# The first half of a mixture-of-experts feed-forward made sparse: tokens sorted into 15 slot tiles, ahead of a dense second half

## The chip, the cores and the metric

The kernel runs on one core of one Trainium2 chip, as one program. The metric is the device time of one execution in microseconds (us), taken as the median over several executions. The engines are named as in the profile: PE is TensorE's matmul, PEld its weight load, DVE is VectorE, ACT is ScalarE, POOL is GpSimd, SP issues the DMAs. A q behind a name (PEldq) means the sequencer of that engine, which executes register instructions and sends the others on.

## The reference, cut to what matters

Three blocks follow each other on 1024 tokens of width 128: a bidirectional Mamba2 block, a cross attention of the 1024 tokens (8 heads) to 6404 context rows and themselves, and a feed-forward with 8 experts of hidden width 512, of which each token uses two. Only the last one changes:

```python
logits = xn @ router_w                       # 1024 x 8
topv, topi = jax.lax.top_k(softmax(logits), 2)
topv = topv / topv.sum(-1, keepdims=True)
comb = sum(one_hot(topi, 8) * topv[..., None], axis=1)
out = 0
for e in range(8):                           # every expert for every token, most with weight 0
    out = out + comb[:, e:e + 1] * swiglu(xn, gate_up_w[e], down_w[e])   # 128 -> 2 x 512 -> 128
out = out + swiglu(xn, shared_gate_up_w, shared_down_w)                  # 128 -> 2 x 128 -> 128
# swiglu: gate, up = split(x @ gu); silu(clip(gate, -10, 10)) * up @ dn
x = layernorm(x + out)
```

## The kernel before, in words

Each engine has an instruction list written out by hand, and semaphores order them. Every product of the feed-forward is made of three float16 matmuls (high x high, high x low, low x high).

**The attention** works through 16 blocks (head x half of the tokens, NBLK = 16), each of 30 steps (NS = 30). A step is six matmuls of 512 columns for the scores, two exponentials on ACT (`weights`), the low part on DVE (`low`), and, two steps later, six matmuls of 512 columns for the values. In a block, steps 0 to 6 and 25 to 29 (TAIL = 25) are written out, and steps 7 to 24 are a hardware loop of three turns (`Fori`). The addresses in these loops depend on registers, which FUSED_REGOPS and ALU_OP instructions of the PE sequencer work out between the matmuls. The last block (`end=True`) has no work for a following one, and carries the layer norm, the transposed copy and the routing of the first 512 tokens (`half_norm`, `turned`, `route`, in `half_in_block`).

**The feed-forward** runs over two halves of 512 tokens. A half is a shared unit, then 8 experts of 4 units each (hidden width 4 x 128), so 66 units in all. A unit u goes through a fixed chain:

- PE `gate_up`: three matmuls of 512 columns for the gate (bank u % 2), three for the up part (bank 2 + u % UPS, with UPS = 3). The gate waits until `clip` of unit u - 2 has read its bank, the up part until `hidden` of unit u - 3 has.
- DVE `clip` (L1447), ACT `silu` (L900), DVE `hidden` (L1455), ACT `high` (L906), POOL `hidden_low` (L617).
- An expert's down products are 4 tiles of 12 matmuls with 128 columns (`down`), two steps or more behind, into a ring of three banks (DOWNS = 3). DVE's `down_acc` (L1464) weighs each and adds it to `acc`, and frees its bank.

DVE's own order is: `clip(u)`, the tiles of the step before, `hidden(u - 1)`, then a piece of side work: the norm and routing of the second 512 tokens during the first half, the final norm of the first 512 during the second. PE places tiles behind the gate or the up part of given units (`tiles_at`): unit 0 of an expert has two, unit 1 none, units 2 and 3 one each. All PE matmuls are recorded under L1569.

Of the kernel before, what the change touches and what calls it, by code (L numbers as in the profile page):

```python
# [23 lines left out]
P = 128  # L24
# [32 lines left out]
UPS = DOWNS = 3  # L57
# [7 lines left out]
UNITS = 1 + 4 * E  # L65


def unit_of(half, e, i):

    return UNITS * half + 1 + 4 * e + i  # L70


def tile_of(half, e, t):

    if half:
        return 42 + 4 * e + t
    return 4 + 4 * e + t if isinstance(e, int) and e == 0 else 9 + t if isinstance(e, int) and e == 1 else 6 + 4 * e + t


def shared_tile(half, t):  # L80

    return 38 * half + t


TURNED, ROUTED = 8, 13
NTILES = tile_of(1, E - 1, HT - 1) + 1
ALL_TILES = range(HT)


def tiles_at(half, e, i):  # L90

    plain = {0: ([("own", -2, 2)], [("own", -2, 3)]), 1: ([], []), 2: ([], [("own", -1, 0)]), 3: ([], [("own", -1, 1)])}
    first = {(0, 0): {0: ([], []), 2: ([("shared", 0, 0)], [("shared", 0, 1)]), 3: ([("shared", 0, 2)], [("shared", 0, 3)])},
             (0, 1): {0: ([], [])},
             (0, 2): {1: ([], [("turned", 0, 0)])},
             (0, 3): {1: ([], [("routed", 0, 0)])},
             (1, 0): {0: ([], []), 1: ([], [("other", E - 1, 0)]), 2: ([], [("other", E - 1, 1)]),
                      3: ([("other", E - 1, 2)], [("other", E - 1, 3)])},
             (1, 1): {0: ([("shared", 0, 0)], [("shared", 0, 1)]), 1: ([("shared", 0, 2)], [("shared", 0, 3)])}}
    return first.get((half, e) if isinstance(e, int) else None, {}).get(i, plain[i])  # L100


BEFORE_SHARED = ([("other", E - 2, 2)], [("other", E - 2, 3)])
# [34 lines left out]
def layer(nc, a, out):  # L138
    ctx = ExitStack()
    with ctx:  # L140
# [47 lines left out]
        xf_1 = take([HT, D])  # L188

# [6 lines left out]
        U_sb = take([2, QB])  # L196

# [5 lines left out]
        A = take([4, 4, QB], F16)  # L203

# [118 lines left out]
        dn_ps, dn_acc, last_lo = sem("dn_ps"), sem("dn_acc"), sem("last_lo")  # L323
# [108 lines left out]

        def stage_parts(par, dst):
# [13 lines left out]
        def _(sp):  # L447
# [11 lines left out]
            loads(sp, ld_fv, fv)  # L459

# [5 lines left out]
            for e in range(E + 1):  # L466
# [17 lines left out]
        def _(pool):  # L484
# [130 lines left out]
            def hidden_low(u, k, lo, hi):  # L615
                pool.wait_ge(f_hi, u + 1)
                g.tensor_tensor(lo, hid[:, k % RING], hi, ALU.subtract).then_inc(f_lo, 1)  # L617

            def expert_low(half, e, par, blocks=4):
                for i in range(blocks):  # L620
                    hidden_low(unit_of(half, e, i), half + 1 + i, hlo[:, par, i], hhi[:, par, i])

            for half in range(2):
                hidden_low(UNITS * half, half, slo, shi)
                with pool.Fori(0, E // 2 - half) as pair:
                    for par in range(2):
                        expert_low(half, 2 * pair + par, par)
            for e in (E - 2, E - 1):
                expert_low(1, e, e % 2, 4 if e < E - 1 else 3)
# [3 lines left out]
        def _(act):  # L633
# [128 lines left out]
            def joint_act(h):  # L762
# [4 lines left out]
                if h:  # L767
                    act.wait_ge(ah_lo, h)
                s.activation(AH32[:], b[:, 0], ACT.Copy, scale=scale).then_inc(ah_f32, 1)
# [84 lines left out]
            def block_act(j, first=False, nxt=True, end=False):  # L854
# [6 lines left out]
                with act.Fori(0, LOOPN) as i:  # L861
                    for k in range(6):
                        weights(j, Turn(i, k))
# [1350 lines left out]
```

## Time and profile before

| | |
|---|---|
| median of 3 runs | 1809.35 us (1807.37 to 1809.6) |
| profiled execution | 1806.91 us, span of its instructions 1805.2 us |
| busy share of the span | PE 96%, DVE 83%, ACT 62%, PEld 48%, POOL 15% |
| last attention block | 1557 to 1660.6 us of the span |
| feed-forward, first half on PE | 1660.68 to 1726.1 us |
| feed-forward, second half on PE | 1726.1 to 1796.7 us |
| granted TensorE clock, mean | 0.991 |

Rows of the timeline give the start, the length, and how many like instructions were merged. A merged row's length ends with the modelled end of its last matmul, which lies behind the start of the next row: the distance of starts is the rate. A row of one source gives, per instruction and tile, the count, the shortest, median and longest duration in ns, and the first and last start.

### The profile page before, as it was taken

The page shows a single profiled execution, that of the slowest core. Times are in us where ns is not written, and L with a number is a line of the kernel's source. Part 1 is how long each engine was busy: PE and PEld are TensorE (multiplying, and loading weights), DVE is VectorE, ACT ScalarE, POOL GpSimd, SP SyncE. Part 2 cuts the span into 40 slices and gives each one's busy share as a digit, 9 for nine tenths or more (in the row PEclk, how much of TensorE's full clock was granted, in tenths as well). Part 3 has the DMA queues.
Part 4 walks back from the last instruction along what each step waited for, and adds up shares of the span by engine and source line. Part 5 has one row for each costly group of instructions (what it writes and reads, how often), then busy time and mean ns, then how long its engine had stood idle before and what let it go on. Part 6 is the DMA issues. An engine that isn't in the chain of part 4 may idle for free. (4 is left out here: it accounts for less than half of the span.)

```text
span 1805.2 us, 31230 instructions
## 1 busy us (share of the span) xinstructions
PE 1739.7 (96%) x9153; PEld 862.3 (48%) x9153; DVE 1492.3 (83%) x2398; ACT 1122.2 (62%) x1374; POOL 274.8 (15%) x340
## 2 busy tenths in 40 slices
PE   6977999999999999999999999999999999999998
PEld 4854444444444444444444444444444444444665
DVE  7968988888888888888878797979787888756987
ACT  4555566666666666666666666666666666676665
POOL 4846991000000000000000000000000000000554
PEclk9989999999999999999999999999999999999999
DMA  4001110000000000000000000000000000000000
GB/s 144 2 1 46 60 40 1 0 0 0 0 0 0 0 0 0 0 0 0 0 0 0 0 0 0 0 0 0 0 0 0 0 0 1 0 1 1 1 8 7
DMA packets 15381, 14.08 MB, mean 8 GB/s; under 512 B 5855, under 2 KB 13795, under 8 KB 14950
## 3 DMA queue, kind: packets, MB, share of 16 engines
q1 hardware_dynamic: 15334, 13.49, 2.5%
q8 instruction: 26, 0.43, 0.1%
q14 instruction: 21, 0.17, 0.0%
HBM read 12.96 MB, written 0.52 MB: 7 GB/s over the span
## 5 line engine op out<-in xcount | busy, mean ns | idle before, releaser
L833 ACT ACTIVATE p_arena<-PS 128x1024 f16<-128x1024 f32 (+1 forms) x480 | 484.4, 1009 | 529.5 <-PE PS L1569 529.3
L1569 PE MATMUL PS<-a_arena,z_arena 128*128 (+1 forms) x2832 | 746.4, 380 | 4.3 <-DVE a_arena L1253 4.1
L1569 PE MATMUL PS<-p_arena,z_arena 128*128 128x512 f16 x2800 | 740.4, 379 | 1.4 <-ACT p_arena L843 0.3
L1266 DVE TENSOR_TENSOR p_arena<-p_arena 128x1024 f16<-128x1024 f32 (+1 forms) x480 | 574.2, 1196 | 110.1 <-ACT p_arena L836 99.5
L1234 DVE TENSOR_REDUCE mxs<-PS 128x512 f32 (+1 forms) x900 | 581.8, 667 | 86.6 <-PE PS L1569 83.2
L836 ACT ACTIVATE p_arena<-PS 128x1024 f32<-128x1024 f32 (+1 forms) x480 | 481.9, 1004 | 0.0
L1569 PEld LDWEIGHTS PS<-a_arena,z_arena 128*128 (+1 forms) x2832 | 275.0, 98 | 332.4 <-DVE a_arena L1253 4.4
L1569 PEld LDWEIGHTS PS<-p_arena,z_arena 128*128 (+1 forms) x2800 | 269.2, 98 | 312.1 <-ACT p_arena L843 8.8
L1569 PE MATMUL PS<-z_arena,a_arena 128*128 (+3 forms) x1024 | 353.9, 361 | 10.5 <-DVE mxs L1234 8.2
L617 POOL TENSOR_TENSOR z_arena<-z_arena 128x512 f16<-128x512 f32 x65 | 75.3, 1160 | 1438.8 <-ACT z_arena L906 1438.5
L1569 PEld LDWEIGHTS PS<-z_arena,a_arena 128*128 (+1 forms) x1024 | 97.9, 98 | 143.7 <-DVE mxs L1234 26.4
L1569 PE MATMUL PS<-w_arena,z_arena 128*128 128x128 f16 (+1 forms) x856 | 67.4, 225 | 6.8 <-DVE w_arena L1110 2.7
L1569 PEld LDWEIGHTS PS<-w_arena,z_arena 128*128 128x128 f16 (+1 forms) x856 | 58.9, 105 | 25.0 <-POOL z_arena L617 5.5
L900 ACT ACTIVATE z_arena<-z_arena 128x512 f32<-128x512 f32 x66 | 41.6, 630 | 33.7 <-DVE z_arena L1447 33.4
L1447 DVE TENSOR_SCALAR z_arena<-PS 128x512 f32<-128x512 f32 x66 | 45.4, 688 | 16.1 <-PE PS L1569 14.6
L906 ACT CAST z_arena<-z_arena 128x512 f16<-128x512 f32 x66 | 40.7, 618 | 15.1 <-DVE z_arena L1455 15.1
L1569 PE MATMUL PS<-z_arena,w_arena 128*128 128x512 f16 x198 | 48.6, 379 | 0.0
L1569 PE MATMUL PS<-wt_arena,w_arena 128*128 128x512 f16 x198 | 48.0, 379 | 0.0
L1455 DVE SCALAR_TENSOR_TENSOR z_arena<-PS,z_arena 128x512 f32<-128x512 f32 x66 | 44.8, 679 | 1.5 <-ACT z_arena L900 1.3
L1569 PE MATMUL PS<-w_arena 128*128 128x64 f32 (+5 forms) x268 | 37.5, 281 | 7.3 <-DVE w_arena L1016 4.5
L1424 DVE TENSOR_REDUCE mxs<-PS 128x2 f32<-128x1024 f32 (+1 forms) x30 | 34.3, 1185 | 10.4 <-PE PS L1569 10.2
L546 POOL TENSOR_SCALAR p_arena<-p_arena,mv,rs 128x127 f32<-128x127 f32 x50 | 41.9, 850 | 0.0
(272 smaller groups left out, 924.0 us busy)
## 6 DMA issues: line engine op xcount, KB each, us to landing
w_arena<-in_L_ffn_gate_up_w SPq DMA_DIRECT2D x8, 512.0 KB, 3.7
p_arena<-in_ctx SPq DMA_DIRECT2D x2, 1600.0 KB, 9.1
w_arena<-in_L_ffn_down_w SPq DMA_DIRECT2D x8, 256.0 KB, 4.0
a_arena<-in_L_xattn_Wkv SPq DMA_DIRECT2D x1, 1024.0 KB, 5.8
w_arena<-in_x SPq DMA_DIRECT2D x1, 512.0 KB, 4.1
a_arena<-in_L_xattn_Wo SPq DMA_DIRECT2D x1, 512.0 KB, 6.8
w_arena<-in_L_xattn_Wq SPq DMA_DIRECT2D x1, 512.0 KB
out<-m_arena SPq DMA_DIRECT2D x4, 64.0 KB, 1.6
```

What stands on the lines that cost most here:

```text
L546: g.tensor_scalar(ctx_sb[:, c, 1:P], ctx_sb[:, c, 1:P], mv[:, c, 0:1], rs[:, 3, c:c + 1], ALU.subtract, ALU.mult).then_inc(z_scaled, 1)
L617: g.tensor_tensor(lo, hid[:, k % RING], hi, ALU.subtract).then_inc(f_lo, 1)
L833: s.activation(Phi[:, r % 3, 0:w], ps, ACT.Exp, scale=1 / SSC).then_inc(hi_ready, 1)
L836: s.activation(P32[:, r % 2, 0:w], ps, ACT.Exp, scale=1 / SSC).then_inc(p32_ready, 1)
L900: s.activation(sil[:, k % RING], gcl[:, k % RING], ACT.Silu, scale=1 / (XS * WS)).then_inc(f_silu, 1)
L906: s.copy(dst, hid[:, k % RING]).then_inc(f_hi, 1)
L1234: v.tensor_reduce(mxs[:, i, bass.ds(kb, 1)], PS[:, 6 + par, 0:w], AX.X, ALU.max).then_inc(mx_read, 1)
L1266: v.tensor_tensor(Plo[:, r % 3, at:w], P32[:, r % 2, at:w], Phi[:, r % 3, at:w], ALU.subtract).then_inc(lo_ready, 1)
L1424: v.tensor_reduce(mxs[:, i:i + 2, kb:kb + 1], PS[:, pair % 2 * 2:pair % 2 * 2 + 2, 0:w], AX.X, ALU.max).then_inc(mx_read, 2)
L1447: v.tensor_scalar(gcl[:, k % RING], PS[:, u % 2], lim, -lim, ALU.min, ALU.max).then_inc(f_clip, 1)
L1455: v.scalar_tensor_tensor(out=hid[:, k % RING], in0=PS[:, 2 + u % UPS], scalar=HS / (XS * WS), in1=sil[:, k % RING], op0=ALU.mult, op1=ALU. ...
L1569: return t.matmul(o, l, r, start=start, stop=stop)
```

## The change

**Sorting.** In the last attention block, the routing of the first half moves from steps 25 to 29 up to steps 7 to 17. New DVE work (`hot`, seven pieces) counts with two small matmuls how many of the 512 tokens, each taken twice, go to each expert, and gives each of the 1024 token copies a row in a list sorted by expert, where each expert's part begins at a multiple of 128. At most 15 tiles of 128 rows come out; all 15 are always worked on. A row holds the token's input (high and low part), its number and its weight (516 bytes). POOL sends the rows to DRAM in 8 indirect DMAs, SP reads them back in 3 DMAs, PE turns them tile by tile. The expert numbers of the 15 tiles are packed into two words that PE loads into registers. Steps 7 to 24 of this block are written out instead of looped. An internal DRAM tensor is set to zero early in the kernel (`xg_zero`).

**The first half.** It is now one shared unit and 15 slot units in a row. A slot unit is all of one expert's hidden width (4 blocks of 128) for 128 rows: 12 matmuls of 128 columns for the gate, 12 for the up part, with the weights at an address made of the expert's register; 12 more for the down product y, also by register; and 8 that scatter y back to the four token tiles through a 0/1 matrix that DVE makes (`choice`), all 15 summed in PSUM bank 7 (COMB). Per two slots, four matmuls turn the rows.

**Around it.** Bank 7 is needed for that sum, so UPS goes from 3 to 2. The second half keeps its matmuls (1 shared and 32 dense units), with tiles at the same places. Before unit 0, DVE does six pieces of the second half's norm. The first half's sum and final norm (`half_done`) follow in five double pieces during units 21 to 25.

```diff
-UPS = DOWNS = 3
+UPS, DOWNS = 2, 3
+COMB = 7
...
+SLOTS = 15
+WEAVE = False
+AHEAD = SLOTS
+def unit_order():
+    order, k = [("shared", 0, 0)], AHEAD
+    order += [("slots", i, 0) for i in range(AHEAD)] + [("shared", 1, 0)]
+    for e in range(E):
+        for i in range(4):
+            order.append(("dense", e, i))
...
+def small_work():
+    for half in range(2):
+        p = at_unit("shared", half)
+        for t in ALL_TILES:
+            put(p + 3 + t // 2, t % 2, "shared", half, t)
+    put(2, 1, "turned", 1, 0)
+    put(5, 1, "routed", 1, 0)
+    for f in range(2, (SLOTS + 1) // 2):
+        put(at_unit("slots", 2 * f) - 4, 1, "rows", f, 0)
+    for k in range(SLOTS):
+        p = at_unit("slots", k)
+        put(p + 3, 0, "y", k, 0)
+        put(p + 5, 1, "comb", k, 0)
+    for e in range(E - 1):
+        p = at_unit("dense", e, 3)
+        for t, (step, part) in enumerate(((3, 1), (4, 1), (5, 0), (5, 1))):
+            put(p + step, part, "own", e, t)
...
@@ gpsimd
+            for k in range(2):
+                for t in ALL_TILES:
+                    g.indirect_dma_start(xg_dram, bass.IndirectOffsetOnAxis(ap=posu[:, k, t:t + 1], axis=0),
+                                         xrow_f[:, k, t, :], None).then_inc(sent, 16)
@@ sync
+            sp.wait_ge(sent, 16 * 2 * HT)
+            for k, r in enumerate(SLOT_PARTS):
+                sp.dma_start(xg_f[:, r.start:r.stop, :],
+                             xg_dram.rearrange("(i p) n -> p i n", p=P)[:, r.start:r.stop, :]).then_inc(xg_ld[k], 16)
@@ vector
+                elif kind == "y":
+                    choice(a)
+                    dve.wait_ge(y_hi, a + 1)
+                    v.scalar_tensor_tensor(out=yw[:, a % 3, 1], in0=PS[:, bank, 0:P], scalar=xg_f[:, a, D + 1:D + 2],
+                                           in1=yw[:, a % 3, 0], op0=ALU.mult, op1=ALU.subtract).then_inc(dn_acc, 1)
...
+            for piece in range(6):
+                half_norm(1, piece)
+            for u in range(NUNITS):
+                clip(u)
+                if u:
+                    for kind, a, t in work_at(u - 1, 0) + work_at(u - 1, 1):
+                        small_dve(kind, a, t)
+                    hidden(u - 1)
+                side_work(u)
@@ tensor, last block
+                        if st == 10:
+                            pe.wait_ge(cnt_ready, 1)
+                            mm(PS[:, 6, 0:HT * E], J32[:], of_all)
+                            mm(PS[:, 6, HT * E:2 * HT * E], ones[:], of_all).then_inc(hot_ps, 1)
+                        elif st == 12:
+                            half_rows(xfhi[0], 7).then_inc(hot_ps, 1)
+                        elif st == 13:
+                            half_rows(xflo[0], 6).then_inc(hot_ps, 1)
...
+                    if st == TAIL and end:
+                        pe.wait_ge(hot_read, 3)
+                        for f in range(2):
+                            slots_turned(f, 6 + f).then_inc(xt_ps, 1)
+                    if st == TAIL + 3 and end:
+                        pe.wait_ge(et_ready, 1)
+                        packs.extend(t.value_load(packu[0:1, i:i + 1], min_val=0, max_val=E ** E - 1) for i in range(2))
@@ tensor, feed-forward
+            expert = [(packs[k // E] >> (3 * (k % E))) & (E - 1) for k in range(SLOTS)]
+            def free_bank(u, o):
+                if o == 0 and u >= 2:
+                    pe.wait_ge(f_clip, u - 1)
+                if o == 1 and u >= UPS:
+                    pe.wait_ge(f_hid, u + 1 - UPS)
+            def slots_products(u, o, blk, bank):
+                k = ORDER[u][1]
+                hi, lo = (w[:, bass.ds(expert[k] * (2 * F) + (F * o + blk * P), P)] for w in GU_flat)
+                c = bank[:, blk * P:(blk + 1) * P]
+                mm(c, hi, xt[:, k, 0], stop=False)
+                mm(c, hi, xt[:, k, 1], start=False, stop=False)
+                last = mm(c, lo, xt[:, k, 0], start=False)
```

## Rows read from the trace of the kernel before

**Rows 1.** The page's busy line, and one stretch of the chain (start, length)

```profile
PE 1739.7 (96%) x9153; PEld 862.3 (48%) x9153; DVE 1492.3 (83%) x2398; ACT 1122.2 (62%) x1374; POOL 274.8 (15%) x340
...
1740.58 46.92 PE PS L1569 x432
```

**Rows 2.** Busy time by stretch: the last attention block, the first half; PE, PEld, DVE, ACT, POOL, PEclk

```profile
1557.00:1660.60 103.60, 99.98 (x493) 48.61 (x492) 60.08 (x113) 71.51 (x77) 0.00 (x0) 1.00 0.00 1
1660.60:1726.00 65.40, 62.74 (x536) 38.49 (x535) 58.20 (x156) 42.16 (x69) 35.33 (x31) 1.00 0.00 1
```

**Rows 3.** What PE waited for, 1660 to 1700 us, then 1700 to 1790

```profile
PE PS L1569 <- POOL z_arena L617: 1.2, 2, 0.7
PE PS L1569 <- DVE acc L1464: 0.9, 1, 0.9
...
PE PS L1569 <- POOL z_arena L617: 0.6, 1, 0.6
```

**Rows 4.** Timeline of PE in the feed-forward: tiles of 12 narrow matmuls between wide ones

```profile
1701.10 0.83 PE L1569 MATMUL PS<-w_arena,z_arena 128*128 128x128 f16 x12
...
1701.77 0.81 PE L1569 MATMUL PS<-wt_arena,w_arena 128*128 128x512 f16 x3
...
1702.41 0.83 PE L1569 MATMUL PS<-w_arena,z_arena 128*128 128x128 f16 x12
```

**Rows 5.** Two sources by operation, 595.9 to 596.8 us: PE's sequencer in an attention loop

```profile
L1569 PEldq FUSED_REGOPS  x6: 46/46/60, 596.0 to 596.6; - x6
...
L1879 PEldq ALU_OP  x1: 32/32/32, 596.7 to 596.7; - x1
```

**Rows 6.** Timeline of an expert's units 1 and 2 in the second half

```profile
1747.30 2.75 PE L1569 MATMUL PS<-z_arena,w_arena 128*128 128x512 f16 x12
...
1748.22 0.69 DVE L1447 TENSOR_SCALAR z_arena<-PS 128x512 f32<-128x512 f32 x1
1748.83 0.60 DVE L1464 SCALAR_TENSOR_TENSOR acc<-PS,wt_arena,acc 128x128 f32<-128x128 f32 x2
1749.34 0.68 DVE L1455 SCALAR_TENSOR_TENSOR z_arena<-PS,z_arena 128x512 f32<-128x512 f32 x1
```

**Rows 7.** Timeline of the start of the feed-forward

```profile
1660.68 4.70 PE L1569 MATMUL PS<-wt_arena,w_arena 128*128 128x512 f16 x21
...
1661.61 0.68 DVE L1447 TENSOR_SCALAR z_arena<-PS 128x512 f32<-128x512 f32 x1
...
1664.03 0.86 DVE L1290 BATCH_NORM_STATS2 st<-acc 128x6 f32<-128x128 f32 x4
...
1666.13 0.37 DVE L1294 BATCH_NORM_AGGREGATE mv<-st 128x2 f32<-128x6 f32 x4
```

**Rows 8.** Small DVE operations of the norm, in order (1749.94 us and on)

```profile
1749.94 0.15 DVE L1305 TENSOR_TENSOR rs<-wt_arena 128x4 f32<-128x4 f32 x1
1750.13 0.16 DVE L1306 TENSOR_TENSOR rs<-rs,wt_arena 128x4 f32<-128x4 f32 x1
```

**Rows 9.** Timeline of steady steps in the last attention block

```profile
1601.26 1.46 PE L1569 MATMUL PS<-a_arena,z_arena 128*128 128x512 f16 x6
...
1603.68 1.02 ACT L836 ACTIVATE p_arena<-PS 128x1024 f32<-128x1024 f32 x1
1603.85 1.46 PE L1569 MATMUL PS<-a_arena,z_arena 128*128 128x512 f16 x6
1604.73 1.23 DVE L1266 TENSOR_TENSOR p_arena<-p_arena 128x1024 f16<-128x1024 f32 x1 [1.36 <-ACT p_arena L836]
```

**Rows 10.** DMA issues: KB each, median us to landing

```profile
w_arena<-in_x SPq DMA_DIRECT2D x1, 512.0 KB, 4.1
...
out<-z_arena SPq DMA_DIRECT2D x4, 64.0 KB, 1.6
```

**Rows 11.** Groups by operation, 1660 to 1806 us (busy, mean ns, idle before)

```profile
L617 POOL TENSOR_TENSOR z_arena<-z_arena 128x512 f16<-128x512 f32 x65 | 75.3, 1160 | 1438.8 <-ACT z_arena L906 1438.5
...
L1569 PEld LDWEIGHTS PS<-w_arena,z_arena 128*128 128x128 f16 x792 | 49.2, 98 | 21.5 <-POOL z_arena L617 5.5 <-issue 2.0
```

More of the change, by code:

```diff
@@ L64 @@
 HT = TC // 2
[L65 to L86, printed above, removed]
-ALL_TILES = range(HT)
[L90 to L100, printed above, removed]
@@ L103 @@
-BEFORE_SHARED = ([("other", E - 2, 2)], [("other", E - 2, 3)])
+ALL_TILES = range(HT)
+SLOTS = 15
+WEAVE = False
+ROW = 2 * D + 4
+AHEAD = SLOTS
[5 more added lines that the diff above has]
+            order.append(("dense", e, i))
+            if i % 2 == 0 and k < SLOTS:
+                order.append(("slots", k, 0))
+                k += 1
+    return order
@@ L106, in is_latent, with number, work_at @@
+WORK = small_work()
+BANKED = [w for at in sorted(WORK) for w in WORK[at] if w[0] != "comb"]
+NSMALL = len(BANKED)
+COMB_END = at_unit("slots", SLOTS - 1) + 6
+def number(kind, a, b=0):
+    return BANKED.index((kind, a, b))
+def work_at(step, part):
+    return WORK.get((step, part), [])
 def is_latent(chunk):
@@ L946, in _ @@
+            high(LAST_UNIT)
             root(4)
@@ L1549, in _, with half_done @@
-            for t in (2, 3):
-                expert_acc(1, E - 2, t)
+            def half_done(piece):
+                if piece == 0:
+                    dve.wait_ge(comb_ps, SLOTS)
+                    dve.wait_ge(dn_acc, number("shared", 0, HT - 1) + 1)
+                    for t in ALL_TILES:
+                        last = v.tensor_tensor(acc[:, t, :], acc[:, t, :], PS[:, COMB, t * P:(t + 1) * P], ALU.add)
+                    last.then_inc(comb_read, 1)
+                    dve.wait_ge(comb_read, 1)
+                    half_norm(0, 0, twice=False)
+                elif piece < 4:
+                    half_norm(0, 2 * piece - 1, twice=False)
+                    half_norm(0, 2 * piece, twice=False)
+                else:
+                    half_norm(0, 7, twice=False)
@@ new lines, in ready @@
+            def ready(u):
+                kind, a, i = ORDER[u]
+                if (kind, a) == ("shared", 0):
+                    pe.wait_ge(stage_used, NPART * E + 2)
+                elif (kind, a) == ("shared", 1):
+                    pe.wait_ge(xf_hi, 2)
+                    pe.wait_ge(xf_lo, 2)
+                elif kind == "slots":
+                    if a >= 4:
+                        pe.wait_ge(dn_acc, number("rows", a // 2) + 1)
+                    elif u < 2:
+                        pe.wait_ge(xt_sb, 2)
@@ new lines, in dense_product @@
+            def dense_product(u, o, n, bank):
+                kind, a, i = ORDER[u]
+                half = a if kind == "shared" else 1
+                at = FS * o if kind == "shared" else i * P + F * o
+                hi, lo = (w[:, at:at + P] for w in ((SGhi, SGlo) if kind == "shared" else (GUhi[:, a], GUlo[:, a])))
+                last = mm(bank, (hi, hi, lo)[n], (xfhi, xflo, xfhi)[n][half], start=n == 0, stop=n == 2)
+                if n == 2:
+                    last.then_inc((f_gate, f_up)[o], 1)
@@ L2176, in _ @@
-            for t_ in range(HT):
+            gate_done = False
+            for u in range(NUNITS):
+                if not gate_done:
+                    plain(u, 0)
+                small_work_pe(u, 0)
+                gate_done = WEAVE and u + 1 < NUNITS and (ORDER[u][0] == "slots") != (ORDER[u + 1][0] == "slots")
+                if gate_done:
+                    woven(u)
+                else:
+                    plain(u, 1)
+                small_work_pe(u, 1)
+            for u in range(NUNITS, NUNITS + 6):
+                for part in range(2):
+                    small_work_pe(u, part)
```

608 lines of the change are left out of this document (373 added, 235 removed).

## The prediction

> **What bounds the kernel now.** I read the page's busy line first, then the busy time by stretch, the chain, PE's waits, and the timelines around the stages that the change touches. PE is busy for 96% of the span, at its full clock in both stages that matter [rows 1, 2]. The chain that ended last runs through PE alone for 47 us of the feed-forward [rows 1]. The first half loses only 2.7 us to waits on PE: 1.2 and 0.6 for the low part from POOL, 0.9 for a down bank [rows 3]. So the feed-forward costs what PE's matmuls cost, and a change has to be counted in PE's time first. The reader should take two rates from the distance of starts: 12 matmuls of 128 columns take 0.67 us (0.056 each), 3 of 512 columns take 0.64 us [rows 4], and in the attention 12 of 512 take 2.59 us, 0.216 each [rows 9].
>
> **What it removes.** Eight dense experts of the first half, each 24 wide and 48 narrow matmuls: 24 x 0.216 + 48 x 0.056 = 7.87 us, times 8 = 63.0 us. (Check: with the shared unit, the turned and routed tiles, and the waits, less six tiles that run after 1726, this gives about 65, and the half lasts 65.4 [rows 2].) The 2.7 us of waits go too. Sum -65.7 us.
>
> **What the 15 slot units cost.** By matmuls a slot has 12 + 12 + 12 + 8, and two for turning: 46 x 0.056 = 2.58 us, 38.7 us for 15. If that were all, the change would win 24 us. But 36 of the 46 take an address from the expert's register, and the code needs a new address for each high and each low weight: 2 per group of three matmuls, 24 per slot. The attention loop is written in the same way (`scores`: one register address for the high part, used twice, one for the low), and its sequencer rows show the price: six FUSED_REGOPS and the ALU_OP behind them start within 0.7 us, though each takes 46 ns [rows 5]. That is 0.12 to 0.13 us from one to the next, with the matmuls in between. There it is hidden, because each matmul takes 0.216 us. Behind matmuls of 0.056 us it is not: three of them give 0.17 us of work, their two addresses take 0.25. I take 24 x 0.125 = 3.0 us, and 0.4 us for the expert's number and for three or four waits that come in pairs and need an instruction of their own at the same rate. A slot is then bound by PE's sequencer at 3.4 us; 15 make 51.0 us. From below, it is the 2.58 us of matmuls; from above, address instructions of 60 ns instead of 46 [rows 5], 3.7 us, 56 in all.
>
> The other engines stay below 3.4 us per slot. DVE has clip and hidden at 0.61 each from start to start, y's second part as one `acc` step of 0.3 (two take 0.60) [rows 6], the choice matrix at most like a clip, 0.6, and half a turned pair, 0.3: 2.4 us. POOL has one low part of 1.16 us [rows 11].
>
> The Trainium skill ("TensorE: Matmul & The Clock Gate", section "Back-to-back issue gap") says that a stream of weight loads and matmuls sustains about 81 ns per 128 columns and 131 ns per 512. By it a slot's matmuls would take an estimated 3.7 us and a dense expert 7.0, and 15 slots would save nothing over 8 experts even without addresses. This trace disagrees: 56 and 216 ns [rows 4, 9].
>
> **What the start costs.** DVE now does six pieces of norm before the first clip: 0.86 for the statistics, 0.65 for the second piece [rows 7], then four of three small operations at 0.19 [rows 8], together 3.8 us. The first clip moves from 1661.6 [rows 7] to 1665.4 and ends at 1666.1. PE has done the shared unit and a slot's gate and up by 1664.1 and may not start the third gate: 2.0 us. Then four norm rows (1.2), the second clip and the first hidden bring hidden(0) to 1668.5, and the third up part, which with two banks needs it, waits 1.3 us. After that the down ring: in steps 3 to 6 up to four tiles share three banks, and a tile waits for an `acc` that stands on DVE behind the clip of the unit whose gate PE has just done. That is 0.17 (0.83 less 0.67 [rows 4]) + 0.69 + 0.3 = 1.2 us; I count 0.7, 1.2, 1.2, and 1.8 where a choice matrix comes first. Sum 2.0 + 1.3 + 4.9 = 8.2 us; 4 if the ring waits overlap with the slow sequencer.
>
> **What two up banks cost in the second half.** Rows 6 show an expert's units 1 and 2 as 12 wide matmuls from 1747.30: the last three, unit 2's up part, start at 1747.30 + 9 x 0.216 = 1749.24. With UPS = 3 they need nothing of unit 0. With UPS = 2 they need its `hidden`, which stands on DVE behind clip(1) and two `acc` steps and ends at 1750.02 [rows 6]. PE waits 0.8 us, in each of 8 experts, and has no idle time elsewhere to give it back: 6.4 us. Nothing would be lost only if DVE had its order changed, which it has not.
>
> **What `half_done` costs.** A dense unit gives DVE 0.61 + 0.61 + 0.3 = 1.5 us of work in about 2.0 of PE. The pieces come doubled now: the first is four adds and the statistics, 2.0 us, the others 0.6 to 1.2, 6 us in five units that have 2.5 us free. With two banks PE can't run far ahead. I take 2.0 us, between 0 and 3.5.
>
> **What the last attention block costs.** A step is 2.59 us of PE; DVE's `low` takes 1.23 of it [rows 9], so the sorting has 1.36 us per step on DVE and may run later than that by some 2.6 us, since the values come two steps behind. Most of it is hidden. PE itself gets 16 narrow matmuls more, 0.9 us. At step 10 it waits for the counts: `low` of step 9 ends 3.4 us after its scores (1604.73 + 1.23, less 1601.26 + 6 x 0.216 [rows 9]), three small operations and a lag of 0.2 make 4.2, and PE is there after three groups of 1.3, 3.9. With the two small float32 matmuls, 0.7 us. At step 28 two registers are loaded, of which no row has a price: 0 if the queued matmuls cover them, twice the 1.6 us of a small DMA's landing [rows 10] as the far bound; I take 1.0. By the Trainium skill ("Runtime: NRT & Kernel Launch", section "Instruction fetch mechanics") a register load costs about 200 ns, so an estimated 0.4; no row here shows it.
>
> The scatter: DVE has the rows ready at about 4.1 us after the scores of step 16, PE wants them turned after those of step 25, 9 x 2.59 = 23.3 us: 19.2 us for eight indirect DMAs in a row on POOL, and the way back. The way back is nearest to the 512 KB load, 4.1 us [rows 10]. That leaves 1.9 us per indirect DMA; a 64 KB store lands in 1.6 [rows 10]. If they cost 2.5 each, PE waits 5 us. I take 0.5. Sum for the block 0.9 + 0.7 + 1.0 + 0.5 = 3.1 us. POOL is idle there [rows 2]; zeroing the DRAM tensor lies early, where PE does not wait for it, and counts nothing, or 1 us if it slows a load. The end of the kernel keeps its order.
>
> **The sum.** -65.7 + 51.0 + 8.2 + 6.4 + 2.0 + 3.1 = +5.0 us. On the profiled execution's 1806.91 that is 1811.9. That execution was 2.4 us under the median of the runs, so against the median, 1809.35, I predict **1814.4 us**.
>
> **Rivals.**
> - *The addresses are hidden (ends faster).* The sequencer works ahead while PE waits, or needs fewer address instructions. Slots then go at 2.6 us, 12.3 us less, of which about 2.5 come back as waits for `hidden` and for POOL's low part: 5.0 - 9.8 = -4.8, 1804.6 us. For it: nothing in the busy line shows the sequencer as a load. Against it: [rows 5], and that each address stands right before its matmul. It decides from a slot below 3.07 us (5.0 / 15 less). Chance 0.17.
> - *The waits are smaller.* DVE gets to `hidden` earlier, the ring waits vanish in the slow slots: 2 to 5 us less, 1809.4 to 1812.4, about 1811. Chance 0.20.
> - *The scatter comes late.* PE stands at step 25 until the rows are back: 5 us more, 1819; worse if an indirect DMA takes over 2.5 us. Chance 0.12.
> - *Weight loads set the pace of narrow matmuls.* PEld takes 98 ns per load [rows 11]; not overlapped, a slot is 46 x 0.098 = 4.5 us, 16.5 more, 1831. Against it: 12 in 0.67 us [rows 4]. Chance 0.02. (The Trainium skill's 81 ns, above, is the milder form of this.)
>
> The forecast itself has 0.49. A measurement of this kernel tells about 0.2% from no change, 3.6 us. Slower by more: most of the forecast (0.38), the late scatter and the loads: 0.52. Within: the smaller waits and the edges of the forecast and of the hidden addresses: 0.31. Faster: most of the hidden addresses: 0.17. The range runs from the hidden addresses to a late scatter with dearer addresses, 1803 to 1822; the forecast's own is 1810 to 1818.
>
> **What would show it.** In the profile after: the distance between clips in the slot units, 3.4 us against 2.6; register instructions of PEldq some 24 per slot at 0.125 us, and PEld idle ended by "issue"; PE's first waits for DVE's clip and hidden, about 2 and 1.3 us; one wait of 0.8 us for `hidden` per expert of the second half; PE without a gap at step 25. A slot below 3.1 us, or no wait for `hidden` in the second half, makes the prediction wrong.

## The result and the profile after

The kernel after takes **1816.94 us** in the median of 5 runs (1816.75 to 1819.94), the kernel before 1809.35 in the runs beside it (1807.37 to 1810.41): a ratio of 1.005, 95% interval [1.0038, 1.0061]. That is slower by 7.6 us, 2.5 us over the 1814.4 forecast and inside the forecast's own range.

The profiled execution took 1819.94 us, with a span of 1818.1. The page's busy line, then the busy time by stretch (last block, first half, second half to 1805, and three short stretches; columns as in [rows 2]):

```profile
PE 1739.8 (96%) x9280; PEld 870.7 (48%) x9280; DVE 1485.7 (82%) x2398; ACT 1105.9 (61%) x1355; POOL 265.5 (15%) x344
```

```profile
1560.00:1665.30 105.30, 101.68 (x515) 50.05 (x513) 67.27 (x139) 71.84 (x78) 9.63 (x20) 1.00 0.05 15
1665.30:1728.80 63.50, 55.89 (x645) 45.71 (x645) 39.89 (x124) 25.81 (x48) 16.93 (x15) 0.92 0.01 2
1728.80:1805.00 76.20, 66.84 (x602) 40.68 (x600) 60.04 (x132) 40.80 (x68) 37.56 (x33) 1.00 0.02 5
1670.00:1675.00 5.00, 3.12 (x26) 2.85 (x27) 4.92 (x12) 2.46 (x4) 1.07 (x1) 0.59 0.00 0
1675.00:1680.00 5.00, 4.76 (x50) 4.19 (x48) 2.15 (x4) 2.03 (x4) 1.34 (x3) 0.73 0.01 3
1690.00:1695.00 5.00, 3.54 (x31) 2.73 (x29) 3.47 (x13) 1.51 (x3) 1.16 (x1) 0.66 0.01 3
```

The busy line hardly differs from [rows 1], and it hides everything: PE's busy time is the same 1740 us, while the first half now holds 645 matmuls at 55.89 us. The granted clock of the first half is 0.92 where [rows 2] have 1.00.

To compare kernels I cut the feed-forward at two events of the timelines: PE's first matmul of the shared unit, and the clip of the second half's shared unit. "First" is the time between them, "second" from there to the end of the span.

| profiled execution | feed-forward starts | second half's clip | span | first | second |
|---|---|---|---|---|---|
| before | 1660.68 | 1726.94 | 1805.2 | 66.3 | 78.2 |
| after | 1665.35 | 1728.85 | 1818.1 | 63.5 | 89.2 |
| before_ups2 | 1664.00 | 1734.20 | 1818.3 | 70.2 | 84.1 |
| static_all | 1664.65 | 1716.45 | 1805.5 | 51.8 | 89.0 |
| static_y | 1665.41 | 1718.91 | 1807.9 | 53.5 | 89.0 |
| norm_spread | 1662.48 | 1720.55 | 1810.8 | 58.1 | 90.2 |
| half_single | 1665.31 | 1728.61 | 1813.3 | 63.3 | 84.7 |
| ups3 | 1662.02 | 1725.18 | 1809.6 | 63.2 | 84.4 |
| hidden_first | 1662.88 | 1730.64 | 1816.7 | 67.8 | 86.0 |
| combo_in_front | 1664.34 | 1724.46 | 1805.7 | 60.1 | 81.2 |

So the sparse half saves 2.8 us, and the dense half, whose matmuls did not change, costs 11.0 more. The last block got 1.4 longer: from the matmul that turns the last maxima (1560.96 before, 1564.27 after) to the start of the feed-forward it takes 99.7 and 101.1. The 3.3 us left between the spans lie ahead of that block, and are no effect of the change: before_ups2 runs the code of before up to the feed-forward and starts it at 1664.00, 3.3 us later than the profiled execution of before. The times of most kernels here fall into two such groups, 2 to 3 us apart, which the medians mix. Each row of the table is one execution, so a stage is compared by this table, and a kernel by its median.

PE's timeline at the start of the feed-forward, then over one slot of the steady part:

```profile
1665.35 1.46 PE L1732 MATMUL PS<-wt_arena,w_arena 128*128 128x512 f16 x6
1666.64 1.50 PE L1732 MATMUL PS<-z_arena,w_arena 128*128 128x128 f16 x24
1667.98 0.39 PE L1732 MATMUL PS<-I,a_arena 128*128 128x128 f16 x4
1671.32 1.46 PE L1732 MATMUL PS<-z_arena,w_arena 128*128 128x128 f16 x12 [2.95 <-DVE z_arena L1607]
1673.34 1.46 PE L1732 MATMUL PS<-z_arena,w_arena 128*128 128x128 f16 x12 [0.56 <-DVE z_arena L1616]
...
1702.93 1.18 PE L1732 MATMUL PS<-w_arena,p_arena 128*128 x12
1703.95 1.14 PE L1732 MATMUL PS<-z_arena,w_arena 128*128 128x128 f16 x12
1704.99 0.38 PE L1732 MATMUL PS<-I,a_arena 128*128 128x128 f16 x4
1705.21 0.61 PE L1732 MATMUL PS<-p_arena 128*128 128x128 f16 x8
```

L1607 is `clip`, L1616 `hidden`. The first two groups take 1.34 us from start to start, what 24 matmuls take without addresses: these had been computed ahead (the address instructions start at 1664.1, while PE is still in the work before them). Then PE stands for 2.95 us until the first clip, and the next 12 matmuls are busy for 1.46 us: the clock is at half. In the steady part no wait is shown, yet each group of 12 takes 1.0 us instead of the 0.67 of [rows 4]. PE counts as busy all the while; only the distance of starts shows the loss. From the clip at 1699.39 to the one seven slots later at 1725.53, a slot takes 3.73 us.

The sequencer's instructions of PE's line, by operation, over 5.5 slots of after, then over six of static_y (below):

```profile
L1732 PEldq FUSED_REGOPS  x132: 46/46/60, 1700.0 to 1720.6; - x132
```

```profile
L1732 PEldq FUSED_REGOPS  x96: 46/46/46, 1700.7 to 1717.1; - x96
```

132 in 5.5 slots are the 24 per slot of the forecast, at the 46 ns of [rows 5].

### The profile page after: what moved, and what is told of

Read it like the earlier page. It is cut to its first block, busy times and chain, and to the rows that moved or that the text cites. A ratio compares the mean times of both kernels' runs of the same rounds, so it can differ in the third digit from the quotient of the medians.

```text
span 1818.1 us, 31500 instructions
## 1 busy us (share of the span) xinstructions
PE 1739.8 (96%) x9280; PEld 870.7 (48%) x9280; DVE 1485.7 (82%) x2398; ACT 1105.9 (61%) x1355; POOL 265.5 (15%) x344
## 4 chain that ended last, share of the span: by engine, by line
PE 87%; DVE 6%; ACT 3%; issue 3%; POOL 1%; DVEq 0%; DMA 0%; SPq 0%; POOLq 0%; ACTq 0%
PE PS L1732 86%; ACT p_arena L931 1%; DVE mxs L1583 1%; DVE mxs L1319 1%; DVE z_arena L1616 1%; ACT p_arena L924 1%; DVE acc L1621 0%; DVE w_arena L1100 0%; DVE w_arena L1274 0%; POOL p_arena L715 0%; POOL z_arena L715 0%; ACT z_arena L767 0%; ACT p_arena L921 0%; DVE m_arena L1280 0%; POOL w_arena L587 0%
## 5 line engine op out<-in xcount | busy, mean ns | idle before, releaser
L1732 PEld LDWEIGHTS PS<-p_arena,z_arena 128*128 128x128 f16 (+1 forms) x2800 | 269.2, 98 | 311.8 <-ACT p_arena L931 8.8
L1732 PE MATMUL PS<-z_arena,w_arena 128*128 128x128 f16 (+1 forms) x558 | 84.0, 287 | 12.9 <-DVE z_arena L1616 9.8
L1607 DVE TENSOR_SCALAR z_arena<-PS 128x512 f32<-128x512 f32 x49 | 33.8, 689 | 38.4 <-PE PS L1732 30.6
L994 ACT ACTIVATE z_arena<-z_arena 128x512 f32<-128x512 f32 x49 | 30.9, 630 | 54.2 <-DVE z_arena L1607 54.2
L1732 PEld LDWEIGHTS PS<-z_arena,w_arena 128*128 (+1 forms) x558 | 43.5, 102 | 35.4 <-DVE z_arena L1616 14.4
L715 POOL TENSOR_TENSOR z_arena<-z_arena 128x512 f16<-128x512 f32 x33 | 38.3, 1160 | 74.3 <-ACT z_arena L1006 74.1
L1732 PE MATMUL PS<-w_arena,z_arena 128*128 128x128 f16 (+1 forms) x472 | 41.0, 230 | 4.7 <-DVE w_arena L1194 2.7
L1583 DVE TENSOR_REDUCE mxs<-PS 128x2 f32<-128x1024 f32 (+1 forms) x30 | 34.1, 1185 | 10.9 <-PE PS L1732 10.8
L1732 PEld LDWEIGHTS PS<-w_arena,z_arena 128*128 128x128 f16 (+1 forms) x472 | 35.1, 112 | 13.1 <-DVE w_arena L1194 3.1
L692 POOL TENSOR_TENSOR w_arena<-w_arena 128x256 f16<-128x256 f32 (+1 forms) x50 | 39.3, 785 | 4.2
```

What stands on the lines that cost most here:

```text
L692: g.tensor_tensor(lo, src, hi, ALU.subtract).then_inc(stage_used, 1)
L715: g.tensor_tensor(lo, hid[:, u % RING], hi, ALU.subtract).then_inc(f_lo, 1)
L994: s.activation(sil[:, u % RING], gcl[:, u % RING], ACT.Silu, scale=1 / (XS * WS)).then_inc(f_silu, 1)
L1583: v.tensor_reduce(mxs[:, i:i + 2, kb:kb + 1], PS[:, pair % 2 * 2:pair % 2 * 2 + 2, 0:w], AX.X, ALU.max).then_inc(mx_read, 2)
L1607: v.tensor_scalar(gcl[:, u % RING], PS[:, u % 2], lim, -lim, ALU.min, ALU.max).then_inc(f_clip, 1)
L1732: return t.matmul(o, l, r, start=start, stop=stop)
```

## The experiments

All edits are to the kernel after, but for before_ups2. Each ratio is to the kernel before, run beside it.

**Addresses, all and in part.**

```diff
-            expert = [(packs[k // E] >> (3 * (k % E))) & (E - 1) for k in range(SLOTS)]
+            expert = [k % E for k in range(SLOTS)]
```

> The expert of slot tile k is the constant k mod 8 instead of the number loaded into a register, so each slot tile uses another expert's weights than it should and none of PE's 24 address instructions per slot is left; matmuls, waits, DMAs and the register load stay. Theory A (PE's sequencer sets the pace of the slots, 24 addresses at about 0.125 us): a slot falls from the 3.76 us measured after the change to 2.6 to 2.8 (46 matmuls at 0.056), 15 slots give back 14 to 17 us, 1800 to 1803 us, and groups of 12 matmuls take 0.67 instead of 1.05. Rival B (weight loads of 98 ns, or DVE with its clip, hidden, choice and y, set the pace): a slot stays at 3.5 to 3.8, 1813 to 1817 us.

1808.32 us, 0.9994 [0.9985, 1.0003]; the first half is 11.7 us shorter. The median lies above the expected 1800 to 1803 and below rival B's 1813 to 1817.

```diff
-                    his, los = ([w[:, bass.ds(expert[a] * (4 * D) + i * D, D)] for i in range(4)] for w in DN_flat)
+                    his, los = ([w[:, bass.ds((a % E) * (4 * D) + i * D, D)] for i in range(4)] for w in DN_flat)
```

> Only the down weights of the slots have fixed addresses (expert k mod 8); gate and up keep the register, so 16 of 24 address instructions per slot are left and the down products use another expert's weights. As the prediction priced it (one total per slot: addresses x 0.125 us, the sequencer works ahead over the matmuls that need none), a slot loses 1.0 us down to about 2.8, 15 us in all, 1802 us. If the sequencer does not work ahead and only the group of 12 itself gets shorter (1.05 to 0.67), a slot loses 0.38, 5.7 us in all, 1811 us. By rival B of the run with all addresses fixed: no change, 1817.

1806.12 us, 0.9986 [0.9977, 0.9995]; the first half is 10.0 us shorter. PE's timeline of one slot in static_y, then of two groups in static_all:

```profile
1700.83 1.04 PE L1732 MATMUL PS<-z_arena,w_arena 128*128 128x128 f16 x12
1701.81 0.83 PE L1732 MATMUL PS<-w_arena,p_arena 128*128 128x128 f16 x12
1702.48 0.83 PE L1732 MATMUL PS<-z_arena,w_arena 128*128 128x128 f16 x12
1703.15 0.61 PE L1732 MATMUL PS<-p_arena 128*128 128x128 f16 x8
1703.59 1.12 PE L1732 MATMUL PS<-z_arena,w_arena 128*128 128x128 f16 x12
```

```profile
1698.05 0.83 PE L1732 MATMUL PS<-z_arena,w_arena 128*128 128x128 f16 x12
1698.72 0.83 PE L1732 MATMUL PS<-w_arena,p_arena 128*128 128x128 f16 x12
```

Without addresses every group takes 0.67 us: weight loads and PE itself are no limit, and rival B falls. (By the 81 ns per narrow matmul of the Trainium skill, "TensorE: Matmul & The Clock Gate", section "Back-to-back issue gap", these 12 would take an estimated 0.97; the trace disagrees once more. That the forecast's estimate from that figure, 3.7 us a slot, is what after takes is a coincidence: without addresses a slot takes 2.85.) With y's addresses gone, y takes 0.67, and so does the group behind it (1702.48 to 1703.15), though it kept its 8 addresses: the sequencer computed them during y. It works ahead by about one group. The group that has 8 unaddressed matmuls ahead of it still takes 1.03. Over seven slots a slot is 2.84 us (19.90 / 7), 0.89 less for 8 addresses, 0.111 each: the total per slot decides, as in the forecast, not the single group. (Two of the three groups in static_y run at PE's own rate, so if the sequencer stood still now and then behind them, an address costs more than 0.111; no run settles that.)

static_all comes to 2.85 and not to 2.6. Late in its steady slots DVE is nearly full (columns as in [rows 2]), and some groups of 12 start 0.9 us apart; once PE waits 0.73 us for POOL:

```profile
1705.00:1710.00 5.00, 4.98 (x90) 4.80 (x87) 4.90 (x11) 2.67 (x6) 2.32 (x2) 1.00 0.01 3
```

The expected 14 to 17 us became 12 mostly at the start. From the first matmul to the ninth clip static_all takes 29.2 us and after 34.0, 4.9 less; the seven slots behind it give 6.2. In the first slots PE's waits for DVE are about as long as in after (2.67 for the clip, then 0.76, 0.98, 0.98 and 1.37). In the medians static_all isn't faster than static_y, though its profiled halves are 1.7 us shorter; that stays open.

**Two up banks, by themselves.**

```diff
-UPS = DOWNS = 3
+UPS, DOWNS = 2, 3
```

> The kernel before with two up banks instead of three and nothing else changed (three down banks, dense halves). The prediction's term, 0.8 us per dense expert of four units: 16 x 0.8 = 12.8 us more, 1822; with the 0.89 measured after the change, 14 more, 1823. Rival (the wait for hidden after the change comes from the slots' other work, not from the banks): 0 to 3 more, 1809 to 1812.

(The bank of one of the last tiles moves from 3 to 7 with it.) 1819.41 us, 1.0049 [1.0035, 1.0063]: alone in the kernel before, two banks cost as much as the whole change. The second half gets 5.9 us longer, the first 3.9. Together that is less than the expected 12.8: the experts of the first half lose less than 0.8 each. Clips at the ends of one steady expert, in before and in after:

```profile
1773.52 0.68 DVE L1447 TENSOR_SCALAR z_arena<-PS 128x512 f32<-128x512 f32 x1
...
1781.38 0.68 DVE L1447 TENSOR_SCALAR z_arena<-PS 128x512 f32<-128x512 f32 x1
```

```profile
1783.98 0.68 DVE L1607 TENSOR_SCALAR z_arena<-PS 128x512 f32<-128x512 f32 x1
...
1792.62 0.68 DVE L1607 TENSOR_SCALAR z_arena<-PS 128x512 f32<-128x512 f32 x1
```

7.86 against 8.64 us (before_ups2 has 8.64 too): 0.78 per expert. The 0.89 in my expectations was a misreading; the forecast's 0.8 was right. PE's wait for `hidden` itself is 0.6 us there, here in after:

```profile
1801.39 0.82 PE L1732 MATMUL PS<-z_arena,w_arena 128*128 128x512 f16 x3 [0.60 <-DVE z_arena L1616]
```

**A third up bank where one is free.** From unit 22 on, the bank of the slots' sum serves.

```diff
+        THIRD = 22
+        def up_bank(u):
+            return 2 + u % 2 if u < THIRD else (2, 3, COMB)[(u - THIRD) % 3]
...
+                if o == 1 and u == THIRD + 2:
+                    pe.wait_ge(comb_read, 1)
+                elif o == 1 and u >= 2:
+                    pe.wait_ge(f_hid, u - 1 if u < THIRD + 3 else u - 2)
```

> From unit 22 on (the dense units of the second half from expert 1 on, when the sum of the slots has been read) the bank of that sum serves as third up bank. Theory A (PE's wait for hidden is the price of two up banks, 0.89 us per expert measured after the change): the distance of an expert's clips goes back from 8.65 to 7.8 us in about 7 experts, and part of the 4.7 us of the stretch with the doubled norm pieces goes too: 6 to 10 us less, 1807 to 1811. Rival (DVE is late in these units whatever the banks are, and PE then waits for clip at the gate instead): 0 to 2 us less, 1815 to 1817.

1812.87 us, 1.0024 [1.0015, 1.0034], between the two expected ranges; second half 4.8 us shorter, its steady experts back at 7.86. Theory A holds for the steady experts. The stretch with the doubled norm pieces keeps its 13.34 us. The third bank comes into use at unit 24, within this stretch; from there PE's waits for `hidden` (1.13, 0.68 and 1.28 us in after) give way to waits for an addition (0.73), a clip (1.03) and POOL (1.16), so DVE is late there with three banks too. Whether three banks would shorten the units before has no run.

**The doubled norm pieces.**

```diff
-                    half_norm(0, 0, twice=False)
-                elif piece < 4:
-                    half_norm(0, 2 * piece - 1, twice=False)
-                    half_norm(0, 2 * piece, twice=False)
...
+                    half_norm(0, piece - 1, twice=False)
...
-                elif 0 <= u - COMB_END < 5:
+                elif 0 <= u - COMB_END < 9:
```

> The closing norm of the first half goes one piece per unit, in nine units, instead of doubled in five. Theory A (doubled pieces make DVE late by more than the banks hide: 13.3 us for four units instead of 8.65): 2 to 3 us less, 1814 to 1815. Rival (with two up banks each unit already waits for hidden, so every piece of DVE work ahead of it costs its full length wherever it stands): no change, 1816 to 1818.

1815.26 us, 1.0035 [1.0022, 1.0049], 1.7 us less in the median; by the profiled executions, which start the feed-forward at nearly the same time (1665.35 and 1665.31), the second half is 4.5 us shorter. The four units that took 13.34 us take 8.35. The kernel after shows why, in DVE's and PE's timeline of that stretch (other rows between them left out):

```profile
1742.64 0.87 DVE L1669 TENSOR_TENSOR acc<-acc,PS 128x128 f32<-128x128 f32 x4
...
1743.55 0.87 DVE L1375 BATCH_NORM_STATS2 st<-acc 128x6 f32<-128x128 f32 x4
1744.45 0.69 DVE L1607 TENSOR_SCALAR z_arena<-PS 128x512 f32<-128x512 f32 x1
1745.06 0.68 DVE L1616 SCALAR_TENSOR_TENSOR z_arena<-PS,z_arena 128x512 f32<-128x512 f32 x1
...
1745.80 0.82 PE L1732 MATMUL PS<-z_arena,w_arena 128*128 128x512 f16 x3 [1.55 <-DVE z_arena L1616]
```

Clip and hidden stand behind 1.8 us of side work, PE waits 1.55, and since it stood, DVE can't get ahead again for the next pieces. The rival (each piece costs its full length wherever it stands) falls.

**The norm ahead of the first clip.** One piece per unit from unit 0 to 7; `turned`, the low part and the routing follow six units later.

```diff
-    put(2, 1, "turned", 1, 0)
-    put(5, 1, "routed", 1, 0)
+    put(8, 1, "turned", 1, 0)
+    put(11, 1, "routed", 1, 0)
...
-                if u == 0:
-                    half_norm(1, 6)
-                    half_norm(1, 7)
+                if u < 8:
+                    half_norm(1, u)
...
-            for piece in range(6):
-                half_norm(1, piece)
```

> The norm of the second half goes to DVE one piece per unit from unit 0 to 7, as in the kernel before, not six pieces ahead of the first clip; its turned tile, its low part and its routing follow six units later. Theory A (the six pieces cause PE's first wait, 2.95 us, and this idle time is what the half clock of 6.8 us behind it follows from): the first clip comes 3.8 us earlier, the wait shrinks to under 0.5, the half clock (3.4 us lost) goes: 5 to 7 us less, 1810 to 1812. Rival (the clock falls because of the thin stream of narrow matmuls, or the pieces only move into the slots and delay their clips): 0 to 3 us less, 1814 to 1817, and a granted clock of 0.5 somewhere in the first slots.

1815.23 us, 1.0035 [1.0021, 1.0048]; first half 5.4 us shorter, second 1.0 longer. PE's start, and its first half as one stretch (columns as in [rows 2]):

```profile
1662.48 1.46 PE L1728 MATMUL PS<-wt_arena,w_arena 128*128 128x512 f16 x6
...
1665.34 0.83 PE L1728 MATMUL PS<-z_arena,w_arena 128*128 128x128 f16 x12
```

```profile
1662.40:1720.50 58.10, 53.75 (x646) 43.02 (x645) 38.89 (x116) 23.63 (x45) 16.99 (x15) 1.00 0.01 2
```

No wait for the clip, and the granted clock is 1.00 throughout, although PE still waits 1.04 and 1.14 us for additions and 1.46 us for y's second part on DVE. The thin stream of narrow matmuls does not lower the clock by itself; that part of the rival falls. The median gained only 1.7 us, which is the rival's range; this profiled execution is of the earlier group, after's of the later one, and the two halves together say 4.4. If the four runs of 1815.2 to 1815.9 are the later group, as 1819.94 is in after, each group gained about 4.

**DVE's order.** The forecast said that two banks would cost nothing only if DVE had its order changed.

```diff
                 clip(u)
                 if u:
+                    hidden(u - 1)
                     for kind, a, t in work_at(u - 1, 0) + work_at(u - 1, 1):
                         small_dve(kind, a, t)
-                    hidden(u - 1)
```

> On DVE the hidden product of unit u - 1 comes right behind the clip of unit u, and the down tiles' additions after it, not before it; two up banks stay. Theory A (PE's third up part waits for a hidden that stands behind two additions of 0.3 us each): the wait of 0.89 us per dense expert falls to 0.2 to 0.4, so 4 to 5 us less over eight experts, and some more in the stretch with the doubled norm pieces: 1811 to 1813 us; the slots keep 3.76. Rival (the additions, now later, hold the three down banks, and PE waits for them instead): 0 to 2 us less, 1815 to 1817.

1818.43 us, 1.0055 [1.0042, 1.0069]. Steady experts fall from 8.64 to 8.12, as theory A has it, and the second half is 3.2 us shorter. But the first half is 4.3 longer, and the median lies above both expected ranges. Its waits (PE, 1662 to 1700 us), and two stretches of it:

```profile
PE PS L1732 <- DVE acc L1621: 3.3, 2, 1.7
PE PS L1732 <- DVE z_arena L1607: 2.9, 1, 2.9
PE PS L1732 <- DVE p_arena L1647: 2.1, 1, 2.1
```

```profile
1680.00:1685.00 5.00, 3.99 (x41) 3.77 (x39) 2.87 (x4) 0.73 (x3) 1.15 (x1) 0.66 0.00 0
1685.00:1690.00 5.00, 4.33 (x37) 4.08 (x38) 2.54 (x7) 1.33 (x3) 1.15 (x1) 0.69 0.01 3
```

The 2.9 us for the clip are in after too. The rival's waits (an addition, now late, holds a down bank) appear where the slots start: 1.58 us up to 1679.72 and 1.68 up to 1685.67, in after one of 1.08. Behind each of them the clock falls to half, where after has 1.00 from 1678 to 1691. Both theories are right, each in its own stage.

**Slots between dense units, plain and woven.** `AHEAD = 4`, then also `WEAVE = True`.

> Only four slot tiles stand ahead of the dense half; the other eleven come one after every second dense unit, gate, up and down each in a stretch of its own. Theory A (PE's sequencer works ahead, so the addresses are computed while PE does the wide matmuls of dense units): eleven slots fall to about 2.6 to 2.9 us, 9 to 12 us less, and more because DVE gets to hidden between them: 1804 to 1808. Rival (the sequencer can only run ahead by a few matmuls, so each group of 12 with addresses still takes 1.05): 0 to 4 us less, 1813 to 1817.

> As the run with four slots ahead, and where a slot stands beside a dense unit, three wide matmuls of the dense unit are put between the groups of three narrow ones of the slot. A block then has 0.17 + 0.22 us of matmuls over two addresses of 0.125 each. If the sequencer can run ahead only by a few matmuls, this hides the addresses of gate or up of eleven slots where the unwoven order does not: 11 x 0.76 = 8 us less than that order, about 1806. If it runs ahead far, both orders are the same within 2 us.

Plain 1818.33 us, 1.0045 [1.0031, 1.0059]; woven 1808.75, 0.9993 [0.9984, 1.0002]. The feed-forward, 152.7 us after the change, takes 151.9 plain (1664.88 to the end) and 142.0 woven (1665.92). PE's timeline around a plain slot, then what PE waited for from 1700 to 1800:

```profile
1729.60 0.83 PE L1732 MATMUL PS<-w_arena,z_arena 128*128 128x128 f16 x12
1730.27 0.83 PE L1732 MATMUL PS<-z_arena,w_arena 128*128 128x128 f16 x12
1730.94 1.06 PE L1732 MATMUL PS<-w_arena,p_arena 128*128 x12
```

```profile
PE PS L1732 <- DVE z_arena L1616: 9.9, 8, 2.3
```

The addressed group at 1730.27 takes 0.67, so its addresses were hidden behind unaddressed work, and theory A is right in that; y behind it has them in the open again. By its time neither theory came. PE's busy time over the feed-forward falls by 2.7 us only (127.1 in after, 124.3), and its waits take that back: 10.9 us for `hidden` and 3.1 for additions, against 9.8 and 1.3. Woven, the waits for `hidden` fall to 5.5 us, and the busy time to 120.6. So of the 10 us between the two orders more than half are waits; it is not the addresses alone that the weaving hides.

**The repairs together, in front and woven.** combo_in_front has norm_spread, half_single, ups3 and hidden_first. combo_woven has them with `AHEAD = 8` and `WEAVE = True` (norm over units 0 to 4, third bank from unit 36); combo_woven_old_order is that without hidden_first.

> All 15 slots ahead as in the change, with four repairs together: norm of the second half spread over units 0 to 7, closing norm of the first half in single pieces, third up bank from unit 22 on, hidden ahead of the additions. In the profiles the feed-forward was shorter by 4.4 us with the first, 4.7 with the second, 5.2 with the third. If these are separate losses they add up: 14 us less, 1803 us. If they are one loss (a late hidden under two banks) counted three times in the second half: 4.4 + 5 to 7, 1806 to 1808 us.

1808.40 us, 0.9997 [0.9988, 1.0006], just above the range for one loss counted three times; but by the halves it is 11.4 us less, of the 14.3 that the first three add up to. hidden_first, which is in it too, lost 1.1 over both halves when alone. The second half shows separate losses: 8.0 us less, where the three add up to 8.3. The shortfall is in the first half, 3.4 less where they add up to 5.9. There PE waits 2.12 and 1.74 us for additions, and the second wait is followed by half clock, as in hidden_first. No run has the three in front without it.

> The same four repairs (norm pieces over units 0 to 4, third up bank from unit 36 on), with eight slots ahead and seven behind dense units, their gate or up blocks woven with wide matmuls of the dense unit. If a woven slot costs PE its matmuls alone (2.7 us instead of 3.76), 7 us less than the combination with all slots in front, 1796 to 1801 us. If the two up banks that 19 more units have to share give it back as waits for hidden, as with four slots ahead and no weaving: the same as that combination, 1803 to 1808 us.

**1803.11 us, 0.997 [0.9959, 0.9981]**: faster than both kernels; its feed-forward takes 135.0 us (from 1665.16) against 144.5 before. It meets the edge of the second expectation: 5.3 us less than with all slots in front, where the woven matmuls alone would have given 7.

> The woven combination with DVE's old order (additions ahead of hidden), the other three repairs kept. In the run of the order alone the dense experts became 0.53 us shorter each, and the first slots lost 6 us (waits of 1.7 us for a down bank, and half clock behind them). Theory A (the order does harm where slots start and the good it does is there only as long as two up banks are shared): 3 to 7 us less than the woven combination with the new order, 1796 to 1800 us, the 4.2 us wait for an addition gone. Rival (with two up banks in units 9 to 35 the old order costs 0.5 to 0.9 us per four units, some 5 us, in waits for hidden): no gain over 1803.

1803.10 us, 0.9967 [0.9955, 0.9979]; feed-forward 136.2. The two orders are even, so the rival holds, and hidden_first is not needed for the gain. Two losses stay in both. Where the slots start, PE waits 4.22 us for an addition (3.39 with the old order), with the doubled norm pieces of units 2 to 4 on DVE; no run takes that apart. The other, here in combo_woven, is at the routing of the second half:

```profile
1709.27 1.28 ACT L947 ACT_TABLE_LOAD   x1
...
1710.79 1.28 ACT L1035 ACT_TABLE_LOAD   x1
...
1712.84 0.69 DVE L1623 SCALAR_TENSOR_TENSOR z_arena<-PS,z_arena 128x512 f32<-128x512 f32 x1 [1.22 <-ACT z_arena L1001]
...
1713.88 1.17 PE L1734 MATMUL PS<-w_arena,p_arena 128*128 x12 [2.15 <-DVE acc L1628]
```

ACT loads a table for the exponential and another for silu; the silu is late, then `hidden`, then the addition whose down bank PE needs. With the old order the wait of 2.31 us there is for `hidden`. No run moved these loads, so that they are the cause is a reading of the trace.

## Why the prediction was right, point by point

- **Removed work** (-65.7) was not measured by itself; the halves below are counted against it.
- **15 slots** (+51.0): the mechanism held, the size was short. 15 x 3.73 = 56.0, so 5.0 more (3.73 is the mean of seven slots without a wait; the first eight, with their waits, were not priced by themselves). The term that was mis-sized is the 0.4 us beside the addresses. An address costs 0.111 us by static_y, not 0.125; 24 make 2.7, and 1.1 is left for issuing the rest. Even at 0.125 each, 0.7 would be left. By the upper bound I gave, 3.7 a slot, it would have been right.
- **The start** (+8.2): the first half fell by 2.8 us and not by 65.7 - 51.0 - 8.2 = 6.5; with 5.0 for the slots that leaves 6.9. That is a remainder, and its parts were other ones. PE's waits in the first half:

```profile
PE PS L1732 <- DVE p_arena L1647: 1.5, 1, 1.5
PE PS L1732 <- DVE acc L1621: 1.1, 1, 1.1
PE PS L1732 <- POOL p_arena L715: 1.0, 1, 1.0
```

  The clip wait was 2.95 (forecast 2.0) and hidden 0.6 (1.3). Of the four ring waits two came, much as I had them: 1.08 for an addition (1.2), and 1.46 for a y behind a choice matrix (1.8; L1647 is y's second part). They make 2.5 in place of 4.9, and POOL's 1.0 is added. The waits sum to 7.3, already more than 6.9, and the half clock, which I did not foresee, comes on top; so a part is given back, since the sequencer computes addresses while PE waits. What the clock costs by itself isn't separated: norm_spread, without half clock and with 4.0 us of waits, is 5.4 shorter, which leaves about 2 for it; ups3, with the half clock at the start but not the one at 1690, is only 0.3 shorter.
- **Two up banks** (+6.4): 5.9 by before_ups2, 0.78 per steady expert. Right.
- **`half_done`** (+2.0, bounds 0 to 3.5): 4.5 by half_single, above the bound. I had subtracted the free time of five units; once PE stands, that free time is gone. The second half's last 0.6 us has no experiment.
- **The last block** (+3.1): 1.4. The 16 narrow matmuls (0.9) are there; the turned rows go through at 1645.64 without a wait, so the scatter was in time. An indirect DMA lands in 2.4 us in the median, more than the 1.9 that I allowed, but POOL starts the next one after 1.3, before the last has landed; all eight are issued in 10.7 us. (Each moves 128 rows of 520 bytes: 2 x 128 values in float16 and two in float32. The 516 in the part on the change is a slip.) The two register loads take 0.30 and 0.49 us on PE's sequencer (1651.5 to 1652.9), and PE has no wait there; the forecast had 1.0.

The DMA issues, POOL's and PE's timeline of after:

```profile
xg_dram<-z_arena,a_arena POOLq DMA_INDIRECT x8, 2.4
...
1634.63 0.96 POOL L709 DMA_INDIRECT xg_dram<-z_arena,a_arena  x1 [0.30 <-issue]
1635.89 1.02 POOL L709 DMA_INDIRECT xg_dram<-z_arena,a_arena  x1 [0.31 <-issue]
...
1645.64 0.61 PE L1732 MATMUL PS<-I,a_arena 128*128 128x128 f16 x8
```

The terms are then -65.7 + 56.0 + 6.9 + 5.9 + 4.5 + 0.6 + 1.4 = +9.6, twice the forecast's 5.0. (6.9 and 0.6 are remainders, so that the sum meets the two halves and the last block proves nothing.) On 1806.91 that is 1816.5. The forecast then added 2.4 us, the distance of that execution from the median; four of after's five runs (1816.75 to 1817.23) lie in its own earlier group and do not have them. So two errors, 4.6 short and some 2 over, partly cancelled: that the forecast came within 2.5 us is partly luck. What decides the group of an execution is open.

Of the rivals, hidden addresses needed a slot under 3.07 us; it was 3.73. The smaller waits came true for the ring and for hidden alone, the late scatter did not, and static_all rules out the weight loads.

## What to carry to other kernels

Count a sequencer's address instructions before making matmuls narrow: at 0.11 us each they need about two narrow matmuls of cover, and unaddressed work put between them gives a part of it. Look at what an edit takes from the stages that it doesn't rewrite: here one bank and a few small pieces on DVE cost more in the untouched half than the sparse half saved. Where several small losses come from different stages, repair them together; each of the four alone left the kernel slower than before, three of them with the weaving made it faster.

## What the runs showed of the hardware

- **Half clock after an idle stretch.** At the end of PE's 2.95 us wait the granted clock fell to 1.2 GHz (0.50 of full speed from 1671 to 1677; 0.59 and 0.73 over two stretches of 5 us), and PE was busy 1.46 us with 12 narrow matmuls, not 0.83. With the wait gone, in norm_spread, the level stayed at 2.4 GHz. The wait thus cost more than its length. The length of a wait alone doesn't decide it: behind a wait of 1.46 us the clock fell in after (0.66 at 1690) and did not in norm_spread (1.00), and behind one of 1.37 us it fell in static_y and did not in static_all.
- **PE's sequencer works ahead by about one group of 12 matmuls.** An addressed group right behind an unaddressed one takes 0.67 us (static_y, ahead4); the next takes 1.0.
- **A matmul can be late without an idle time.** In the steady slots PE shows 4.95 to 4.98 of 5 us busy, at 60 to 67 matmuls per 5 us, where static_all has up to 94.
